# Four-layer graph network on one core: source blocks of 256 edges instead of 512, two pairs of sum banks, and the edge network's sum on ScalarE and GpSimd

## The reference

```python
xs = x[:, :C] @ W_in2f_s ; xv = (x[:, C:] as n,C,3) @ W_in2f_v       # C = F = 128: the table z, 512 wide
sj, vj = xs[dst], xv[dst]                                            # gathered for each edge
u = r_ij / norm(r_ij) ; Yv = Y1_SCALE * u
h = softplus(f_ij @ Wf1 + bf1) - log(2)                              # edge network, f_ij has 20 features
W = (h @ Wf2 + bf2) * rcut_ij[:, None]                               # 512 columns of it are used
m_s = stack(sj * Y0, sum_i vj*Yv) * W[:, :2F]
m_v = stack(sj * Yv, vj * Y0) * W[:, 2F:4F, None]                    # message: 1024 wide
agg = segment_sum(concat(m_s, m_v), src, num_segments=n)
S = softplus(agg_s @ W1_s) @ W2_s ; V = (agg_v @ W1_v) @ W2_v
x = layernorm(x + concat(S, V))
```

## Time and profile before

| | |
|---|---|
| median of 3 runs | 2405.64 us (2403.09 to 2406.53) |
| profiled execution, its own time | 2401.41 us |
| its span, first to last instruction | 2399.7 us |
| mean granted TensorE clock | 0.916 of full speed |
| edge loop | about 1345 to 2350 us of the span, 88 groups |

### The profile page before, as it was taken

One profiled execution on the slowest core, in us unless ns is written; L12 is line 12 of the kernel. 1 busy time (PEld: TensorE's weight loads), 2 busy tenths in 40 slices (PEclk: granted clock), 3 DMA queues, 4 the chain that ended last, 5 costly groups with the idle time before them and its releaser, 6 DMA issues.

```text
span 2399.7 us, 39923 instructions
## 1 busy us (share of the span) xinstructions
PE 2170.3 (90%) x8194; PEld 1250.7 (52%) x8194; DVE 1648.2 (69%) x4611; ACT 1262.7 (53%) x3671; POOL 1284.6 (54%) x1637
## 2 busy tenths in 40 slices
PE   3896595788879999999999799999999999999997
PEld 3453242666765545455444555555555555555555
DVE  8998524999996060101413688888888888888885
ACT  0496776777773010000110576666766767666664
POOL 1578576666666566640000566666666666666650
PEclk9698898555567999999999899999999999999999
DMA  5200211111112111110000333333333333333331
GB/s 191 70 3 3 87 22 16 15 15 15 14 15 61 33 37 15 15 50 0 22 19 1 103 100 98 97 102 94 100 99 96 102 96 99 98 98 102 95 97 43
DMA packets 72826, 146.45 MB, mean 61 GB/s; under 512 B 23565, under 2 KB 36098, under 8 KB 72391
## 3 DMA queue, kind: packets, MB, share of 16 engines
q0 software_dynamic: 46080, 103.42, 17.6%
q1 hardware_dynamic: 23740, 36.99, 4.6%
q10 hardware_dynamic: 2946, 5.28, 0.6%
HBM read 122.80 MB, written 22.30 MB: 60 GB/s over the span
## 4 chain that ended last, share of the span: by engine, by line
PE 74%; DVE 16%; issue 4%; ACT 3%; DVEq 1%; DMA 1%; POOL 0%; ACTq 0%; SPq 0%; POOLq 0%
PE ps L838 26%; PE ps L587 11%; PE ps L606 7%; PE ps L824 4%; PE ps L779 4%; PE ps L826 3%; PE ps L827 3%; PE ps L825 3%; PE ps L737 3%; PE ps L679 2%; ACT dense L955 2%; DVE dense L1320 2%; DVE adj_t L1342 2%; DVE dense L1319 2%; DVE adj_t L1157 2%
## 5 line engine op out<-in xcount | busy, mean ns | idle before, releaser
L838 PE MATMUL ps<-adj_t 128*128 128x512 f32 x1408 | 671.4, 599 | 0.1
L482 POOL DMA_INDIRECT src_table<-st_rec,st_idx x320 | 386.8, 1209 | 272.7 <-DMA st_rec<-records 177.7
L1044 ACT ACTIVATE adj_t<-adj_t 128x128 f32<-128x128 f32 x1056 | 344.6, 389 | 218.3 <-DVE adj_t L1496 217.1
L529 POOL DMA_INDIRECT adj_t<-z_table,adj_t x352 | 339.1, 963 | 168.2 <-DVE adj_t L1506 79.8
L838 PEld LDWEIGHTS ps<-adj_t 128*128 128x128 f32 x1408 | 253.6, 189 | 257.0 <-issue 215.0
L470 POOL DMA_INDIRECT pair_table<-dense x160 | 196.8, 1230 | 127.7 <-issue 126.6
L737 PE MATMUL ps<-dense 128*128 128x128 f32 x832 | 254.9, 444 | 0.0
L824 PE MATMUL ps<-dense_r 128*128 128x512 f32 x352 | 217.8, 619 | 2.3 <-POOL dense_r L537 2.3
L737 PEld LDWEIGHTS ps<-dense 128*128 128x128 f32 x832 | 208.9, 308 | 16.8
L606 PE MATMUL ps<-wring,dense 128*128 128x512 f32 (+1 forms) x480 | 208.6, 597 | 4.6 <-issue 3.2
L537 POOL TENSOR_TENSOR dense_r<-adj_t,dense_r 128x512 fp32r<-128x512 f32 x88 | 113.6, 1291 | 170.1 <-ACT dense_r L1053 170.0
(11 more groups left out here) (247 smaller groups left out, 3799.6 us busy)
## 6 DMA issues: line engine op xcount, KB each, us to landing
src_table<-dense SPq DMA_DIRECT2D x8, 704.0 KB, 7.0
adj_t<-src_table SPq DMA_DIRECT2D x88, 64.0 KB, 1.8
adj_t<-z_table,adj_t POOLq DMA_INDIRECT x352, 3.4
src_table<-st_rec,st_idx POOLq DMA_INDIRECT x320, 2.6
records<-dense SPq DMA_DIRECT2D x1, 5000.0 KB
st_rec<-records POOLq DMA_DIRECT2D x80, 62.5 KB, 2.2
wring<-in_edge_attr SPq DMA_DIRECT2D x2, 1562.5 KB
wring<-in_l_w SPq DMA_DIRECT2D x3, 1024.0 KB, 7.6
```

Source lines behind the costliest of these rows:

```text
L482: g.indirect_dma_start(out=src_table, out_offset=bass.IndirectOffsetOnAxis(ap=st_idx[0:EP, k, c:c + 1].bitcast(u32), axis=0), in_=st_rec[0 ...
L529: g.indirect_dma_start(out=zg[:, s, c, :], out_offset=None, in_=z_table, in_offset=bass.IndirectOffsetOnAxis(ap=dsti[:, s, c:c + 1].bitcas ...
L838: last = mm(bank[6 + h], oh[:, c, :], msg[:, c, h * D:(h + 1) * D], start=c == 0, stop=c == GROUP - 1)
L1044: last = A(msg[:, c, (2 + k) * P:(3 + k) * P], msg[:, c, MSG:MSG + P], ACT.Copy, scale=side[:, s, c, C_Y - ATT + k:C_Y - ATT + k + 1])
```

## The change

Four things change together.

- A source block is rounded up to 256 edges instead of 512. The number of places is then 168 pieces (`PAIRS`) of two chunks, 84 groups instead of 88.
- Since a piece is now two chunks, the sums are added after every two chunks, `add_sums(u, k, off)` with u = 0 to 167, from two pairs of banks in turn: banks 4 and 5, and banks 6 and 7. The addition for a group's last two chunks comes after chunk 1 of the next group, that for its first two after its own chunk 3. A single load fetches two columns for both.
- Banks 4 and 5 are taken from `filter_out`, which now has two banks in turn, 2 and 3, and waits for the messages of the chunk two before. In TensorE's order `filter_out(0)` and `filter_out(1)` of g+1 move ahead of `scatter(2)` and `scatter(3)`.
- `hidden` leaves VectorE. ScalarE writes max(u, 0) from bank 1 to `relu_u` between absolute value and exponential (`ACT.Relu`), and GpSimd adds it to the logarithm. That addition stands first in GpSimd's group, ahead of `split`; `filter_in` waits for the Relu instead of `hidden`.

```diff
-QUANT_LOG2 = [7, 9]
+QUANT_LOG2 = [7, 8]
...
-GROUPS = (E + NT * (GROUP * P - 1)) // (GROUP * P)
-GROUPS += GROUPS % 2
+PAIRS = 4 * math.ceil((E + NT * (2 * P - 1)) // (2 * P) / 4)
+GROUPS = PAIRS * 2 // GROUP
...
-SLOTS = [PAIR_CHUNKS, GROUPS]
+SLOTS = [PAIR_CHUNKS, PAIRS]
...
+            def hidden(i, s):
+                gi = 2 * i + s
+                wait_alone(pool, sp_ready, gi + 1)
+                wait_alone(pool, relu_ready, gi + 1)
+                if not (isinstance(gi, int) and gi == 0):
+                    wait_alone(pool, hi_ready, gi)
+                    wait_alone(pool, lo_ready, gi)
+                g.tensor_tensor(h32, relu_u, sp, ALU.add).then_inc(h_ready, 1)
...
             def group(i, s, one=True, two=True):
 
                 nxt = (i, 1) if s == 0 else (i + 1, 0)
+                if one:
+                    hidden(*nxt)
                 if two:
                     split(i + 1, s)
...
-            for c in range(GROUP):
+            gather(0, 0, 0)
+            hidden(0, 0)
+            hidden_lo(0, 0)
+            for c in range(1, GROUP):
                 gather(0, 0, c)
-            hidden_lo(0, 0)
...
-            bU, bW = bank[1], bank[2:2 + GROUP]
+            bU, bW = bank[1], bank[2:4]
...
-                    pe.wait_ge(h_ready, gi)
+                    pe.wait_ge(relu_ready, gi)
...
-                    pe.wait_ge(msg_ready, n - GROUP + 1)
+                    pe.wait_ge(msg_ready, n - 1)
...
-                if c == 0 and not (isinstance(i, int) and gi == 0):
-                    pe.wait_ge(agg_added, gi)
+                u = 2 * gi + c // 2
+                if c % 2 == 0 and not (isinstance(u, int) and u < 2):
+                    pe.wait_ge(agg_added, u - 1)
...
+                if one:
+                    filter_out(*nxt, 0)
                 scatter(i, s, 2)
                 if one:
-                    filter_out(*nxt, 0)
+                    filter_out(*nxt, 1)
                 scatter(i, s, 3)
-                if one:
-                    filter_out(*nxt, 1)
...
                 A(sp, bank[1], ACT.Abs).then_inc(sp_chain, 1)
+                A(relu_u, bank[1], ACT.Relu).then_inc(relu_ready, 1)
...
-                v.scalar_tensor_tensor(h32, bank[1], 0.0, sp, ALU.max, ALU.add).then_inc(h_ready, 1)
...
+            def group(i, s, head=False):
+                u = 2 * (2 * i + s)
+                for c in range(GROUP):
                     one_hot(i, s, c)
+                    messages(i, s, c)
+                    if c == 1 and not head:
+                        at = place_of(u - 1, 2)
+                        add_sums(u - 1, 1, at[0])
+                    if c == 3:
+                        add_sums(u, 0, at[1] if not head else place_of(0, 1)[0])
```

More of the change, by code:

```diff
@@ L1462, in _ @@
             dve.wait_ge(l3w_ready, 2)
-            def hidden(i, s):
-                gi = 2 * i + s
-                dve.wait_ge(sp_ready, gi + 1)
-                if not (isinstance(gi, int) and gi == 0):
-                    dve.wait_ge(hi_ready, gi)
-                    dve.wait_ge(lo_ready, gi)
-                v.scalar_tensor_tensor(h32, bank[1], 0.0, sp, ALU.max, ALU.add).then_inc(h_ready, 1)
             def one_hot(i, s, c):
@@ L1506, in messages, with place_of, add_sums @@
                 v.tensor_tensor(msg[:, c, P:2 * P], vy[:, c, :], b[:, 2 * P:3 * P], ALU.mult).then_inc(msg_ready, 1)
[L1508 to L1512 removed]
+            def place_of(u, count):
+                if count == 1:
+                    return [dve.value_load(src_offs[0:1, ds(u, 1)], min_val=0, max_val=(NT - 1) * MSG)]
+                _, at = nc.values_load_multi_w_load_instructions(
+                    src_offs[0:1, ds(u, count)], engines=[mybir.EngineType.DVE], min_val=0, max_val=(NT - 1) * MSG,
+                    skip_runtime_bounds_check_because="a sum of some of the steps between source blocks; all of them make the last block's place")
+                return at
+            def add_sums(u, k, off):
+                dve.wait_ge(scat_chunk, 2 * (u + 1))
+                if isinstance(u, int) and u == 0:
                     dve.wait_ge(agg_zero, 1)
                 else:
[L1515 removed]
+                    dve.wait_ge(agg_added, u)
                 a = agg[:, ds(off, MSG)]
[L1517 to L1528 removed]
+                v.tensor_tensor(a, a, sums[k][:, :], ALU.add).then_inc(agg_added, 1)
+            def group(i, s, head=False):
+                u = 2 * (2 * i + s)
+                for c in range(GROUP):
+                    one_hot(i, s, c)
+                    messages(i, s, c)
[4 more added lines that the diff above has]
+                        add_sums(u, 0, at[1] if not head else place_of(0, 1)[0])
             group(0, 0, head=True)
@@ L1534, in _ @@
             group(L3_IT - 1, 0)
[L1535 to L1536 removed]
+            group(L3_IT - 1, 1)
+            add_sums(PAIRS - 1, 1, place_of(PAIRS - 1, 1)[0])
             def activated(t):
```

53 lines of the change are left out of this document (18 added, 35 removed).

## The result

The changed kernel takes **2476.4 us** (median of 4 runs, 2473.3 to 2479.0), the kernel before 2405.8: ratio 1.0295, 95% interval [1.0277, 1.0313]. That is 71 us slower. I had said 2413 us and a range up to 2442: the sign was right, the size and the cause were not.

A forecast was written before the change was run, and what follows sets the result against it. TensorE was taken as today's bound, the hidden layer's path as the new one: 84 groups of 11.90 us give +4.3, loop start +2.5, small instructions +0.5, together +7.3 on 2405.6, so 2413 us; range 2380 to 2442.

The forecast's parts named there:

- the sign: Whole kernel: the change makes it slower, given a chance of 0.54, against same 0.20 and faster 0.26.
- Fewer groups: Edge loop: 84 groups instead of 88 save 4 x 11.31 = 45.2 us if TensorE stays the bound.
- The hidden layer's new path: First product to low half via GpSimd: 12.72 us against 11.53 available; TensorE waits every second group, 11.90 us a group.
- VectorE: VectorE's work per group: 11.3 to 11.9 us, under or at 11.90, so hidden, with thin cover.
- The third rival: GpSimd's new addition stops VectorE for all its 1.29 us: 12.6 us a group, 2472 us; chance 0.04.
- the 0.29: L1504 on VectorE: 0.63 us beside L537 instead of 0.34; by the blocking rule, little of 1.29 us was left.
- Two banks for the second product: Second product on TensorE: waiting for messages two chunks back loses its small lead and costs nothing while VectorE is ahead.
- The order of TensorE's work: TensorE's loop: same work in each group as before, 11.31 us.
- TensorE has no gap: Kernel before, edge loop: TensorE busy 997.7 of 1000 us, so a group costs what its instructions cost.
- The loop's start: First groups: later first low half and delayed second path cost together 2.5 us, between 0 and 5.

The follow-up runs named there:

- runs 4, 12: 4: changed kernel, softplus in two ScalarE steps without the sum, 2340.6 us; 12: run 11 with GpSimd's addition behind split and first gather, ratio 0.9762.
- run 11: Changed kernel with VectorE made light: two multiplies on 8 of 128 columns, additions on 128 of 1024; ratio 0.9994 to the kernel before.
- run 5: Kernel before the change with only its edge loop cut to 84 groups; 2361.2 us, ratio 0.9813.
- run 1: Changed kernel with GpSimd's new addition moved behind the split and the first gather; 2463.3 us, ratio 1.0243.
- run 8: Direct softplus kernel (two ScalarE steps, no sum) plus one unread GpSimd addition of 128x512 per group; 2427.0 us, ratio 1.0090.
- run 6: Kernel before, 88 groups and one addition, with only two filter banks and the TensorE order they need; 2495.7 us, ratio 1.0374.
- run 3: Changed kernel with each addition of the sums taking only 512 of 1024 columns; 2420.4 us, ratio 1.0068.
- run 10: Direct softplus kernel with the hidden layer's low half moved from GpSimd to VectorE and its high half earlier on ScalarE; ratio 0.9816 to the kernel before.
- run 2: Changed kernel with the hidden layer's sum back on VectorE and no Relu; 2355.8 us, ratio 0.9791.
- run 9: Direct softplus kernel plus a GpSimd memset of 128x1250 per group, which reads nothing; ratio 0.9879 to the kernel before.

## Why the prediction was wrong

The change has three limits, and the largest decides. All three have now been measured:

| limit | forecast, us to a group | measured |
|---|---|---|
| TensorE's work, new order | 11.31 (a little less in the spread) | 11.04 (runs 4, 12) |
| the hidden layer's path | 11.90 | 11.80 (run 11) |
| VectorE, work and stops | 11.3 to 11.9, "hidden" | 12.63 (changed kernel) |

- *Fewer groups*, -45.2: right, -44.0 by run 5.
- *The hidden layer's new path*, 12.72 us and waits in every second group: the mechanism was right and the size nearly so. In run 11 the path from the first product to the end of `hidden_lo` is 1751.87 to 1764.38, 12.51 us; the same steps of my sum, without the 0.15 to TensorE's start, are 12.57. But it is the second limit. Behind a group of 12.63 us it costs nothing, and run 1 shows that shortening it gives back 0.15 us of 1.6.
- *VectorE*: **this step failed.** I took the instruction that starts at 1756.22 and lasts 0.63 beside GpSimd's `hidden_lo`, and read 0.29 us as the price of GpSimd's presence. But 0.49 us of GpSimd's operation were left when that instruction started, so the row shows only the end of a stop. Caught from the start, such a stop costs 1.0 to 1.3 us in the changed kernel's rows, less where VectorE works from PSUM in the meantime. I also had the undisturbed work too high, at 11.3 instead of 10.67, by taking chunks 2 and 3 as they stood, with a held L1504 in each (0.63 and 0.60 us), and an addition at 1.22 instead of the 1.14 from start to start. The term had to be 10.67 + 2.0 (0.5 us for each of four chunks) instead of 11.3 to 11.9.
- *The third rival* had the mechanism, 12.6 us to a group and 2472 us, and got a chance of 0.04. The mechanism is what happened; that the number fits so closely is in part luck, since 11.3 + 1.29 has work that is 0.6 us too high and stops that are 0.7 us too low against the measured 10.67 + 2.0. The Trainium skill, page "SBUF — State Buffer", section "Who interferes with whom", says that the later of the two stands still until the first is done; the rows of the changed kernel at 1757.58 and 1762.57 agree, where VectorE's instruction starts 0.07 and 0.04 us behind GpSimd's and stands until it is done. In run 8 L1490 also stood until GpSimd was done, 1.42 us longer than it needs, but it is recorded 0.54 us ahead of GpSimd's operation, so that row doesn't tell which of the two was the later. My sentence that the 0.29 "shows how little was left" had the answer in it: when a row can't tell two readings apart and they differ by 34 us, each needs a real chance, or a look at the other rows of the same line.
- *Two banks for the second product*, at no cost: right only together with the second pair of sum banks (run 6). With VectorE full the two banks hand each stop on to TensorE, 69 us of waits for L1513 in 800.
- *The order of TensorE's work* I had left at 11.31. It was worth -0.25 us to a group, 21 us, the only part of the change that gave more than it promised. Some 0.15 of it is a wait for ScalarE in every group of the kernel before, which I had passed over with "TensorE has no gap".
- *The loop's start*, +2.5, between 0 and 5: right, 3.3 us. The first additions, 1365.8 after and 1366.2 before, hide it, since they don't stand behind the same chunk.

With the measured terms the account closes. VectorE's work and stops, 10.67 + 2.00 us, give the measured group of 12.63 to 12.68. 69.0 us in the repeated part and 3.3 at the loop's start are 72.3; the spans differ by 72.0 and the medians by 70.6.

## What to carry to other kernels

Before work goes to GpSimd, list which of VectorE's instructions take all their inputs from SBUF: while a GpSimd operation on a large tile runs, the next of them can stand until it is done. Price it at GpSimd's full length (an operation of 1.28 us cost 1.0 to 1.3 us here, one of 1.06 us cost 1.42), and take it off only where the timeline shows VectorE on PSUM inputs (or idle) at that time. To tell a stop from a stretch, compare ends: many instructions of different lengths that all end at one distance behind the other engine's end were stopped. An engine that is at 87% is not relieved by moving 0.6 us away from it if what comes back is a stop of 1.3 us; with the rest of the change in place, the kernel took 2476 us with the work moved, 2356 with it left on VectorE, and 2341 with it dropped (a softplus in two steps on ScalarE).

When several limits lie within 10% of each other, a part's price depends on the others: the move of the sum cost 29 us alone, by ScalarE's longer path, and 121 us on top of the second addition, by VectorE's stops. And an engine whose recorded lengths leave no gap can still wait: look for a start that always stands at one distance behind another engine's end.

## What the hardware showed

- A stop may begin before GpSimd's operation does in the records. Where an indirect DMA stands right ahead of it in GpSimd's queue, VectorE stood for longer than the operation: L1511 for 1.93 us from 1759.03 although L548 was recorded from 1759.53 to 1760.80 (run 3), L1490 for 1.76 us from 1753.62 although L545 ran from 1754.16 to 1755.22 (run 8). After an idle GpSimd it was 1.38 us for an operation of 1.28. Why the two cases differ is not shown.
- An indirect DMA can have a stop beside it with no large operation of GpSimd near: in the kernel before, L1504 of chunk 3 takes 0.60 us from 1758.41, with only a gather (L529, 1758.13 to 1759.08) recorded beside it, and so in 68 of the 71 groups from 1500 to 2300 us. In run 10, with four gathers to a group, the same multiply has a mean of 344 ns. What makes the difference is not shown.
- The stops move with the phase of the two engines, and need not shrink when VectorE gets more room: 2.0 us to a group in the changed kernel, 2.5 with half additions, but none to speak of in run 2.
- The one-hot's tensor_scalar, which has one tile as input and scalars, is stopped like the multiplies with two tiles, and even by an operation that only writes (run 9). The same section of the Trainium skill counts tensor_scalar among the operations that can take the shared ports and says that two-input instructions clash only with a GpSimd operation that reads; this agrees with run 9 if L1490 stood only behind L1479, which no run here tells apart.
- An extra GpSimd addition of 1.06 us, with no reader and with a third of GpSimd's time free, cost the kernel 86 us, 1.0 us in each of 84 groups.
